# Ten of fifty node chunks moved out of the att2 stage and into the third and fourth layer

## The reference

```
h = maximum(layernorm(x), 0)
x = x + gnn_block(h, edges)
```

## Time and profile before

| | |
|---|---|
| median of 3 runs | 6139.09 us (6133.28 to 6147.22) |
| profiled execution | 6139.83 us, span 6138.10 us |
| busy, share of the span | DVE 68%, POOL 67%, PE 62%, ACT 38% |
| third layer, gathers | 2801 to 3314 us |
| fourth layer, gathers | 3364 to 3881 us |
| att2 | 4894 to 5547 us |

### The profile page before, as it was taken

The page is one execution under the profiler, slowest core; times in us unless marked ns, Lnnn a source line. Parts: engine busy times, 40 slices in busy tenths (PEclk is TensorE's granted clock), DMA queues, the critical chain, the costliest instruction groups (busy, mean ns, idle before and its releaser), DMA issues. The chain is left out here.

```text
span 6138.1 us, 78858 instructions
## 1 busy us (share of the span) xinstructions
PE 3822.7 (62%) x19710; PEld 2610.6 (43%) x19710; DVE 4151.6 (68%) x14950; ACT 2328.9 (38%) x6170; POOL 4084.2 (67%) x4026
## 2 busy tenths in 40 slices
PE   2777788888468868886775555477746557670000
PEld 1444455555245545554554444365635433330000
DVE  6999799999654434443444666566579777776554
ACT  0000477777511111112444555322225489890000
POOL 5777777777767767776775777577700177733776
PEclk9999899999755555555555555577769788995555
DMA  1111344333233323333454354233236567752221
GB/s 40 48 48 48 102 156 150 137 110 104 91 82 102 97 81 102 104 91 99 150 158 137 115 157 145 97 102 102 85 121 228 190 125 146 143 132 78 97 99 66
DMA packets 413631, 685.20 MB, mean 112 GB/s; under 512 B 283685, under 2 KB 290444, under 8 KB 407978
## 3 DMA queue, kind: packets, MB, share of 16 engines
q1 hardware_dynamic: 282410, 542.14, 25.0%
q0 software_dynamic: 130944, 140.05, 12.8%
HBM read 310.94 MB, written 373.78 MB: 112 GB/s over the span
## 5 line engine op out<-in xcount | busy, mean ns | idle before, releaser
L714 POOL DMA_INDIRECT G<-states,srcq x1568 | 1579.0, 1007 | 489.9 <-issue 476.5
L1810 PE MATMUL PS<-ident,HH 128*128 128x128 f32 x2357 | 547.2, 380 | 759.4 <-DVE HH L1308 336.0
L1365 DVE SCALAR_TENSOR_TENSOR R<-R,same,G 128x64 f32<-128x64 f32 x1568 | 448.0, 286 | 763.3 <-DMA G<-states,srcq 584.0
L2085 ACT COPY AT<-PS 128x512 f32<-128x512 f32 (+1 forms) x494 | 284.6, 581 | 1350.8 <-PE PS L1825 864.4
L1810 PEld LDWEIGHTS PS<-ident,HH 128*128 128x128 f32 x2357 | 387.4, 199 | 874.6 <-DVE HH L1308 372.9
L1825 PEld LDWEIGHTS PS<-WD,AT 128*128 128x128 f32 x2358 | 510.5, 319 | 183.6 <-issue 183.2
L827 POOL DMA_INDIRECT out_nodes<-O,dstq x392 | 396.9, 1012 | 276.8 <-DVE O L1145 153.5
L1825 PE MATMUL PS<-WD,AT 128*128 128x64 f32 x2358 | 565.6, 419 | 0.0
L714 POOL DMA_INDIRECT EE<-node_info,srcq x392 | 412.1, 1051 | 133.8 <-issue 133.8
L714 POOL DMA_INDIRECT PG<-in_x,dsti x392 | 406.6, 1037 | 119.4 <-issue 118.5
L714 POOL DMA_INDIRECT G<-states,srci x392 | 404.0, 1031 | 119.4 <-issue 119.4
(11 more groups left out here) (413 smaller groups left out, 10039.5 us busy)
## 6 DMA issues: line engine op xcount, KB each, us to landing
states<-O SPq DMA_DIRECT2D x70, 896.0 KB, 3.8
HH<-states SPq DMA_DIRECT2D x56, 896.0 KB
total<-R SPq DMA_DIRECT2D x56, 896.0 KB, 3.7
XB<-resid SPq DMA_DIRECT2D x42, 896.0 KB, 5.9
states<-HH SPq DMA_DIRECT2D x28, 896.0 KB, 5.0
G<-states,srcq POOLq DMA_INDIRECT x1568, 2.5
resid<-XB SPq DMA_DIRECT2D x28, 896.0 KB, 6.8
xl_of_src<-O SPq DMA_DIRECT2D x14, 1792.0 KB, 6.9
```

Source lines behind the costliest of these rows:

```text
L714: return pool.indirect_dma_start(to, None, table_, bass.IndirectOffsetOnAxis(ap=idx, axis=0), bounds_check=bound, oob_is_err=False).then_i ...
L1365: row = dve.scalar_tensor_tensor(out=R[:, b, j * D:(j + 1) * D], in0=row_before, scalar=same[:, bass.ds(i * C + j, 1)], in1=G[:, b, j * D: ...
L1810: last = pe.transpose(PS[:, 4 + k, q * P:(q + 1) * P], HH[:, b, (g * G4 + q) * D2:(g * G4 + q + 1) * D2], ident[:])
L2085: act.copy(AT[:, k, 0:n * P], PS[:, 4 + k, 0:n * P]).then_inc(s_copied, 1)
```

## The change

Chunks 0 to 9 (20 groups) go through their chain in the third and fourth layer, chunks 10 to 49 stay in att2. The 28 layer chunks are rounds t = 0 to 27 (`CHUNKS * (k - 2) + i`). In round t:

- PE does the units of node round t - 2, one behind each of the slots g = 0 to 4 of `products` (order turn, step0, step1, step2, back), with PSUM banks 1, 2 and 0 in turn; a unit waits for the copy of the unit three before it.
- ACT copies that unit in the same slot, behind `scaled` and `normed_before`; a root at g = 4 in even rounds to 18, and a half of `node_half` (four activations) at g = 5 and another at g = 6 in rounds 1 to 20.
- DVE does `node_stats` behind group 2 in even rounds to 18, `node_scale` there in odd ones, and `node_add` behind group 4 in even rounds from 8 to 26.
- SP loads seven chunks ahead of the third layer's first chunk, and from round 9 in odd rounds stores a chunk (ten in all) and, three times, loads one.

The nodes' buffers in these layers are upper halves of R and O, and parts of EE, SX, XC, SQ, W0, PG and tmp. The counted loops of the two layers on DVE, PE and SP are written out with constants. In att2 45 slots are spread over the 56 places, which leaves 11 places (every fifth) empty, and the flags that ACT makes come every sixth round instead of every eighth. Semaphores for node statistics have names of their own. The diff, cut to its core:

```diff
+        EARLY = 10
+        EARLY_GROUPS = 2 * EARLY
+        NW4 = 4 * NP_
+        upper = [R[:, 0, CD:], R[:, 1, CD:], O[:, 0, CD:], O[:, 1, CD:]]
+        spare = EE[:].rearrange("p k t -> p (k t)")
+        homes = [t[:, NW:NW + NW4] for t in upper] + [spare[:, 4 * NW:4 * NW + NW4], flat[2][:, 400:400 + NW4], flat[2][:, 900:900 + NW4],
...
+        def nodes(k):
+            return IN_LAYERS if k < EARLY else IN_ATT2
+
+
+        def node_units(v, first=EARLY_GROUPS, end=NGROUPS):
 
             made = [("turn", v), ("step0", v - 1), ("step1", v - 2), ("step2", v - 3), ("back", v - 4)]
-            return [(stage, w) for stage, w in made if 0 <= w < NGROUPS]
+            return [(stage, first + w) for stage, w in made if 0 <= w < end - first]
+
+        def early_units(t):
+
+            return node_units(t - 2, 0, EARLY_GROUPS)
...
+        BANKS, EARLY_BANKS = 8, (1, 2, 0)
+
+        def node_bank(n):
+
+            return EARLY_BANKS[n % 3] if n < len(EARLY_UNITS) else (n - len(EARLY_UNITS)) % BANKS
+
+        NSLOTS = NCHUNKS - EARLY + NLAG
+
+        def slots_at(at):
+
+            return range(-(-at * NSLOTS // (4 * CHUNKS)), -(-(at + 1) * NSLOTS // (4 * CHUNKS)))
...
+            def early_nodes(t):
+
+                c = (t - 9) // 2
+                if t % 2 == 1 and 0 <= c < EARLY:
+                    store_nodes(c)
+                    if c + 7 < EARLY:
+                        load_nodes(c + 7)
+
             def layer_program(k, layer):
                 normed = k >= 2
                 kept = 1 + normed
@@ -579,19 +634,33 @@
                     right_in(b, b)
                     if normed:
                         residual_in(b, b)
+                if k == 2:
+                    for c in range(7):
+                        load_nodes(c)
                 body(0, 0, None, first=True)
-                with sp.Fori(0, TURNS - 2) as it:
-                    body(2 * it + 1, 1, it)
-                    body(2 * it + 2, 0, it)
+                if normed:
+                    for i in range(1, CHUNKS - 3):
+                        early_nodes(CHUNKS * (k - 2) + i - 1)
+                        body(i, i % 2, (i - 1) // 2)
...
+                if k == 3:
+                    for j in range(3):
+                        sp.wait_ge(s_nout[j], 16 * len(range(j, EARLY, 3)))
...
+            def early_nodes(t, g):
+
+                if g == 2 and t % 2 == 0 and t // 2 < EARLY:
+                    node_stats(t // 2)
+                if g == 2 and t % 2 == 1 and t // 2 < EARLY:
+                    node_scale(t // 2)
+                if g == 4 and t % 2 == 0 and 0 <= t // 2 - 4 < EARLY:
+                    node_add(t // 2 - 4)
...
                         if g == 1 and between:
                             between()
+                        if normed:
+                            early_nodes(CHUNKS * (k - 2) + i, g)
...
-                    with dve.Fori(0, TURNS - 1) as it:
-                        turn(2 * it + 1, it, 1, it)
-                        turn(2 * it + 2, it + 1, 0, it)
-                    turn(CHUNKS - 1, TURNS - 1, 1, TURNS - 1)
+                    for i in range(1, CHUNKS):
+                        turn(i, i // 2, i % 2, (i - 1) // 2)
...
+            def node_slot(at):
+                for j in slots_at(at):
+                    k = EARLY + j
+                    if j >= 1 and k - 1 < NCHUNKS:
+                        node_scale(k - 1)
+                    if k < NCHUNKS:
+                        node_stats(k)
+                    if j >= NLAG:
+                        node_add(k - NLAG)
...
+                        if beside:
+                            beside(i, g)
...
+            def node_unit(stage, w):
+                n, k = NODE_AT[stage, w], w % 2
+                bank, half, home = node_bank(n), (w % 2) * NW // 2, nodes(w // 2)
+                ring, first = (3, 0) if n < len(EARLY_UNITS) else (BANKS, len(EARLY_UNITS))
+                if n >= first + ring:
+                    pe.wait_ge(s_nput, n + 1 - ring)
+                elif first == 0 and bank == 0:
+                    pe.wait_ge(s_deg, 1)
...
+                def early_nodes(i, g):
+                    units = early_units(CHUNKS * (k - 2) + i)
+                    if g < len(units):
+                        node_unit(*units[g])
+
+                made = products(layer, *how, beside=early_nodes if k >= 2 else None)
...
+            def node_half(k, half, parts=range(2)):
+                act.wait_ge(s_nscales, k + 1)
+                if k >= 2:
+                    act.wait_ge(s_nunit, NODE_AT["turn", 2 * k - 3] + 1)
+                for j in range(half * NC // 2 + parts[0] * NC // 4, half * NC // 2 + (parts[-1] + 1) * NC // 4):
+                    last = act.activation(nodes(k).h[k % 2][:, j * D:(j + 1) * D], nodes(k).x[k % 7][:, j * D:(j + 1) * D], ACT.Relu,
+                                          bias=nodes(k).norms[k % 2][4][:, j:j + 1], scale=nodes(k).norms[k % 2][3][:, j:j + 1])
+                if parts[-1] == 1:
+                    last.then_inc(s_nh, 1)
+
+            def early_nodes(t, g):
+
+                units = early_units(t)
+                if g < len(units):
+                    node_put(*units[g])
+                if g == 4 and t % 2 == 0 and t // 2 < EARLY:
+                    node_root(t // 2)
+                if g in (5, 6) and 1 <= t <= EARLY_GROUPS:
+                    node_half((t - 1) // 2, (t - 1) % 2, [g - 5])
...
                             if i:
                                 normed_before(i, (i - 1) % 2, g)
+                            early_nodes(CHUNKS + i, g)
                         products(layer, copy, put, beside)(i, i // 2, i % 2)
                     normed_last()
                 elif k == 2:
                     for i in range(CHUNKS):
-                        products(layer, copy, put, (lambda i, g: normed_before(i, (i - 1) % 2, g)) if i else None)(i, i // 2, i % 2)
+                        def beside(i, g):
+                            if i:
+                                normed_before(i, (i - 1) % 2, g)
+                            early_nodes(i, g)
+                        products(layer, copy, put, beside)(i, i // 2, i % 2)
```

223 lines of the change are left out of this document (112 added, 111 removed).

## The result

The changed kernel takes 6075.76 us (median of 4 runs, 6072.38 to 6079.68) against 6137.44 of the kernel before: 62 us less. The ratio of the runs is 0.9889, 95% interval 0.9878 to 0.9901 (the two medians alone give 0.9900). The profiled execution took 6077.61 us.

The account below looks back on a forecast made before the run. POOL's gathers were taken to pace both layers, with loops through PE and ACT just under it. Att2 -91, third layer +30 and fourth +16 made -45: 6094 us from 6139.83, range 6045 to 6125.

Parts of the forecast that it names:

- the clock rival: PE's clock rises in the layers as step units join the dense slots; third layer costs 5, total 6069; chance 20%.
- Att2: -91 forecast: Att2: ten chunks (45 slots) leave and the last reduction ends at 5455; -91 us, between -104 and -78.
- 551.5 - 12.3 = 539 us of gathers: Att2: POOL's gathers lose their 12.3 us of waits for a store, take 539 us and end at 5433.
- The sum's lower bound, -104: Att2: largest saving, if slots keep 11.7 us: 45 x 11.7 = 527, plus the last scores.
- The rival that loads of x set the slot: Att2: loads, not the number of chunks, set a slot of 12.8 us; saves 66, total 6119; chance 8%.
- Third layer: +30 forecast: Third layer: node units lengthen the loop through PE at the low clock; +30 us, bounds 5 and 36.
- a full round costs 3.75 over POOL's pace: Third layer: step1, step2 and back add 4.2 us to PE's gapless stretch, less 0.3 and 0.17; rounds 6 to 12: 26.
- The term for the last round, 3.9 into the tail: Third layer: round 13's 3.9 us go into the layer's end.
- Fourth layer: +16 forecast: Fourth layer: node copies and halves lengthen the loop through ACT; +16 us, between 5 and 28.
- 2.8 a round, six rounds: 17: Fourth layer: ACT's loop grows by 3.15 us less 0.33 of room in each full round with halves; 17 us.
- Contention counted as nothing: Both layers: added DVE work lengthens POOL's gathers by 5 us, up to 28, hidden behind a longer loop; counted as nothing.
- Slower because the pauses are not free: Layers: units, copies and node work delay finish, so whole rounds enter the loops; +54 and +75, total 6177; chance 8%.

Follow-up runs that it names:

- scores_apart: Changed kernel with att2's seven additions of gathered rows to the scores each waiting for the one before; 6105.89 us, ratio 0.9941.
- dve_runs: loops_out plus twelve 256-element DVE operations in third-layer chunks 1 to 12, three forms, back to back in odd chunks; 6146.45 us against 6141.99.
- loops_out: Kernel before with only the counted loops of the third and fourth layer written out, no node work moved; 6144.53 us, ratio 1.0004.
- dve_added: loops_out plus DVE products, statistics or one-operand operations in third-layer chunks 1 to 12, each waiting for the one before; 6155.72 us against 6136.64.
- steps_doubled: Changed kernel with each early product of step1 and step2 in the third layer issued twice; 6111.14 us, ratio 0.9906.
- last_chunk_free: units_in_pause with no node work beside the third layer's last chunk, rounds 13 and later one chunk later; 6093.23 us, ratio 0.9896.
- ten_left_out: Changed kernel with the ten early chunks' node chains left out altogether, att2 still doing forty chunks; 6063.39 us, ratio 0.9882.
- units_in_pause: Changed kernel with a round's five node units moved behind PE's groups 0 and 1, into its pause during finish; 6068.81 us, ratio 0.9887.
- last_free_apart: last_chunk_free with att2's score additions each waiting for the one before, as in scores_apart; 6084.65 us, ratio 0.9914.

## Why the prediction was right, and where its terms were off

The direction and the sum's form were right: att2 gives much and the layers take back less. That the total came within 18 us is in part luck, for the terms missed in opposite directions: att2 by 10 us too much saved, the layers by 33 us too much paid (20 and 13). In the third layer the cause was the clock rival's, and the clock's leaving 0.50 there was named as a sign of being wrong. Of the other signs, POOL's wait behind the third layer was 40.43 us and not near 65, and the fourth's 34.37 and not near 48; att2's two came true (no wait for a store, and 15 us from the last gather to the last reduction).

**Att2: -91 forecast, -80.7 measured.** The mechanism is as forecast: gathers without the 12.3 us of waits, and directly behind the last one the landing, addition, leaky step, node addition, product and reduction of the last scores. DVE's timeline of the changed kernel (answers to the earlier trace rows):

```profile
5472.76 0.06 DVE L1706 MEMSET cols<- 128x1 f32 x1 [8.98 <-DMA G<-states_xl,dsti]
5472.85 3.83 DVE L1209 TENSOR_TENSOR HH<-G,HH 128x256 f32<-128x256 f32 x7
...
5483.00 2.02 DVE L1715 TENSOR_REDUCE EE<-HH 128x28 f32<-128x1792 f32 x1
```

The last gather ends at 5537.39 - 67.53 = 5469.86, the last reduction at 5485.02: 15.2 us, where the sum had 2.5 + 12.3 = 14.8. The step that failed is "551.5 - 12.3 = 539 us of gathers". Counted from POOL's first issue of the stage as in the ledger, it had 552.8 - 12.3 = 540.5, and 558.0 came, because the gathers grew from a mean of 1.07 to 1.11 and 1.12 us. One of the long ones, POOL's row and then DVE's:

```profile
5120.82 2.99 POOL L778 DMA_INDIRECT G<-states_xl,dsti  x1 [0.30 <-issue]
```

```profile
5119.00 3.93 DVE L1209 TENSOR_TENSOR HH<-G,HH 128x256 f32<-128x256 f32 x7
```

DVE adds the gathered rows to a scan that it reads across rows, seven operations back to back, and the gather ends 0.9 us behind them. Fourteen gathers of this stage took 1.46 us or more, eleven of them over 2.4; in the kernel before it was eight, one of them over 2.4, and in scores_apart two, none over 2. dve_runs makes such a hold by itself and scores_apart takes it away, so it is shown. But a run need not hold the gather that it meets. In the kernel before, the same runs met gathers nearly as often, 11 of 14 against 13, and one held one, against eleven. One that didn't, DVE's row and then POOL's:

```profile
4973.25 3.90 DVE L1145 TENSOR_TENSOR HH<-G,HH 128x256 f32<-128x256 f32 x7
```

```profile
4975.06 1.32 POOL L714 DMA_INDIRECT HH<-states_xl,dsti  x1 [0.30 <-issue]
```

It starts as far into the run (1.81 us) as the held one above (1.82). What decides stays open. Three further profiles with the kernel before's att2 have six, six and three holds (loops_out, dve_added, dve_runs) and a mean gather of up to 1.09 us, and the other kernels with 40 chunks and these runs six or seven. So the profile from which the 539 us were read was a low one, and some 5 of the 17.5 us lie within such scatter.

The sum's lower bound, -104, doesn't come out of its own terms either: POOL's 5448 allows no more than -98.

The rival that loads of x set the slot was nearer than its 8%. Ten chunks leave two bounds close together: POOL's (gathers plus 67 to 70 us) and the loads'. Where DVE waited 27 to 68 us for x (five kernels with 40 chunks: 27.0, 51.0, 52.4, 58.9, 68.2), att2 took 619 to 626; with 74.9, 81.7 and 108.8 it took 636, 646 and 667.

**Third layer: +30 forecast, +10.0 measured, of which 5 are there without node work.** The step that failed is the 26 us for rounds 6 to 12, that is the clock: "a full round costs 3.75 over POOL's pace" is right for a round at the low clock (40.51 us against 40.4 forecast), but it came once, and the rounds after it ran at 0.69 and 0.70. What the forecast set against this, that "in the layers not one stretch above 0.50", held for the kernel before and not once the units were in; steps_doubled shows it from the other side, with more products and no longer layer. The term for the last round, 3.9 into the tail, measured 6.2 (40.43 - 34.26), and last_chunk_free shows that the round causes it. What was left out is that the gathers took 516 to 519 us in nearly all kernels with the loops written out, with or without node work, against 513.1. What lengthens them stays open, the written-out loops included (dve_added had 514.4, and the fourth layer, in a counted loop before, has the same 517 throughout). The rival of the rising clock had the third layer at 5; its cause was the right one.

The Trainium skill (TensorE: Matmul & The Clock Gate, "Part 1: The HAM clock gate") says that the clock doubles once PE has been kept active. These traces agree in direction, by the layer's mean: 0.50 in the kernel before, 0.59 with the units, 0.63 with two of them doubled, 0.67 with the pause filled.

**Fourth layer: +16 forecast, +2.6 measured.** ACT's loop did lengthen. DVE's rows that wait for the scaled rows (answers to the earlier trace rows):

```profile
3540.83 0.06 DVE L1477 MEMSET cols<- 128x1 f32 x1 [6.11 <-ACT HH L2253]
...
3579.84 0.06 DVE L1477 MEMSET cols<- 128x1 f32 x1 [8.54 <-ACT HH L2253]
```

39.01 us, and 38.1 to 38.3 in four of the other full rounds; forecast were 39 to 40. The term "2.8 a round, six rounds: 17" shrinks to 1.1 to 2.1 over POOL's 36.93 in five distances, 6.9 us together; the six after them, 35.53 to 37.93, win back 2.0 where the forecast had 5. The step that failed is the size of that term; which of its parts was too large wasn't taken apart (PE's granted clock was 0.59 to 0.63 in these rounds). Against ten_left_out the units cost 3.4 in the wait (34.37 against 30.92); in three more profiles of the same placement the wait was 34.8, 37.0 and 38.3, so +2.6 is the low end of what this layer costs. Moving them into the pauses takes that away: 31.0, 31.1 and 31.1 (units_in_pause, last_chunk_free, last_free_apart). So here the placement costs something, but little.

**Contention counted as nothing** holds for the node work in the layers: 14.6 us of statistics a chunk left the gathers at 36.7 to 36.8 us a chunk (dve_added), and in the changed kernel none of the 784 gathers of the two layers took over 1.26 us. It doesn't hold in att2, for the scores' own operations. The Trainium skill (SBUF — State Buffer, "SBUF: two separate sides") says that DVE and GpSimd share one port pair as an exclusive lock and that the loser blocks fully; for DVE operations with two SBUF inputs it says so only against a GpSimd operation that reads SBUF. The traces show such a block for one form alone, 5.83 us behind a run of 6.20, and not each time. For two straight operands there was none: the gathers stayed at 1.03 and 1.04 us. Whether a gather counts as reading SBUF no run shows.

**Slower because the pauses are not free** fell: in units_in_pause three units precede what `finish` waits for, and wherever `finish` waits for ACT the rounds stay at 35.68 to 36.67 us, at a granted clock of 0.59. With the clock low throughout it wasn't tried.

## What to carry to other kernels

A stage stops giving back when the next bound is reached (here ten chunks 81 to 87 us of att2, twenty 91), so a saving per item is not to be multiplied. Whether the first five gave less than half of what ten did isn't shown: some 32 us by the ratio, 21 by profiles of two chips. Work that is added to a TensorE loop at the low clock can't be priced at that clock alone: price both levels and ask which rounds are cold. And an engine that is made faster, as POOL in scores_apart, need not make the kernel faster: the stage's other bound, here DVE with its loads, has to be looked at first. Before a mean from one profile goes into a sum, look how it scatters in other executions of the same code: att2's gathers took 1.07 us in the kernel before and 1.09 in loops_out.

## What the runs showed of the hardware

- DVE operations that read across rows, back to back, can hold a gather that POOL issues until the run ends (5.83 us for a run of 6.20, 2.99 for one of 3.93). They don't do so each time: of the runs of 3.9 us that met gathers, one of 11 held one in the kernel before, 6 of 11 in loops_out, 11 of 13 in the changed kernel. With a wait between the operations none of 24 did (scores_apart and last_free_apart). Straight two-operand and one-operand forms, back to back, did not hold it, nor did statistics with waits between them.
- In the third layer, TensorE's busy time fell from 386.0 to 377.2 us when products were added (steps_doubled), since the granted clock rose from 0.59 to 0.63.
- Loads of 500 KB from the input reached DVE with waits of 27 to 109 us a stage in kernels with the same code in att2, on different chips, and the stage moved by 47 us with them (619 to 667); one profiled execution of such a stage is no measurement of it.
